# Second norm from ScalarE squares, gate batch by batch, batch 0 in the attention tail

## The chip, the core and the metric

The kernel runs on one core of a Trainium2 chip, in one launch. The metric is the device time of that core in microseconds (us). Of the kernel before, three runs gave 1397.35, 1399.73 and 1400.1 us, median 1399.73. The engines are named TensorE (PE), VectorE (DVE), ScalarE (ACT), GpSimd (POOL) and SyncE (SP, which only issues DMAs here).

## The reference, cut to what matters

Two blocks, each added to its input, over B = 4 batches of T = 1024 tokens of C = 128 features in float32.

```
x = x + attn(layernorm(x))            # 8 heads of differential attention, 16 score maps per batch
h = layernorm(x)                      # the second norm
logits = normalize(h) @ normalize(sim) - sigmoid(gates)        # 16 experts
gated  = relu(logits);  mask = gated > 0, or the top 2 where no expert is above 0
rw     = softmax(gated where mask, else -inf)                  # the routing weights
q, k, v = sum_e rw[e] * (h @ W[e])                             # 16 experts, 64 columns each
attn = causal softmax(q k^T / 8) v
x = x + sum_e rw[e] * (attn @ O[e])
```

The second norm needs the finished x of a token, and the gate needs the norm. The first expert product of a token needs its rw.

## The kernel before, in words

The program of each engine is written out by hand, in order, and semaphores join them. An engine whose next instruction waits does nothing behind it.

**Attention** (part one) runs over 256 units (batch, head, block of 128 queries), 32 slots in each of 8 iterations. Per unit TensorE makes two score maps of 128x1024, VectorE takes two negated row maxima (`row_max`, L1246), ScalarE two exponentials (L925), GpSimd scales and adds the two maps (`mix`, L488 and L490; of every eight units ScalarE scales two, L966), TensorE transposes the sum in eight blocks (L632), ScalarE and VectorE copy the two halves out (L854, L332), and TensorE multiplies by the values (L638). Per half of 512 tokens there is a chain: `rows` (transposes), copies and squares, `last`-stage sums, a root on three engines, `norm` on GpSimd (L510), `cols`, `project` (L692), and the addition to `resid` on VectorE (L1278). The slots run on for 21 more after the last unit, to empty this chain.

**Between the parts** the second norm is made for batches 0 to 2 together in those last slots (`ln2_early`): VectorE sums `resid` (L1201), makes the means (L1220), GpSimd and VectorE subtract them (L531, L1204), ScalarE squares 128x1024 at a time (L911), VectorE sums the squares (L1208), then the root and the scaling (L538, L1211). Batch 3 follows when its last half is added. The gate then runs once over all four batches: transposes (`t_ps`, `s_ps`, L721), their split into a float16 high and low part (L991, L1302), the logits (L712), and on VectorE the maxima of each of 32 tiles (L1349), their indices (L1352), the mask and the softmax, up to `rw_all` (L1375). The expert weights are loaded by SP after the last `resid` addition, scaled and split by ScalarE (L1003, L1006) and GpSimd (L548).

**Part two** runs over 32 tiles of 128 tokens. GpSimd multiplies a tile by its 16 weights (`scale_by_experts`, L557, two buffers `xs`: tile m waits for the low part of tile m - 2), ScalarE makes the high part (`x_high`, L1012), VectorE the low part (`x_low`, L1379), SP transposes both by DMA (L427), TensorE multiplies by the 16 experts in four groups (L761), then causal attention one tile behind and two behind, and the output product `y_ps` (L799) four tiles behind. On each engine the steps of several tiles stand in one fixed order per tile; ScalarE's begins with `x_high` of tile m + 2 and the copy of `qkT` (L1032), VectorE's with `x_low` of tile m + 2, and it ends with the low part of `qs` (L1437, L1439), for which TensorE waits at the start of tile m + 1.

Of the kernel before, what the change touches and what calls it, by code (L numbers as in the profile page):

```python
# [40 lines left out]
F16 = mybir.dt.float16  # L41
# [52 lines left out]
EARLY = 3  # L94
POOL_BATCHES = (0, 1)
LN2_SLOT = SLOTS + 1
BT = EARLY * NT
# [50 lines left out]
def block_kernel(nc, x, wq, wkv, wout, lq1, lk1, lq2, lk2, gamma, sim, gates, eq, ek, ev, eo, out):  # L148
    ctx = ExitStack()
    with ctx:  # L150
# [8 lines left out]
        def sem(name):  # L159
# [26 lines left out]
        x2c = prob2.rearrange("p b (t c) -> p (b t) c", c=C)  # L186
        x2sq = prob1[:, 0:4, :]
# [43 lines left out]
        gl = sb("gl", [P, 10, B * NT, E])  # L231
# [3 lines left out]
        rw_all = sb("rw_all", [P, B * NT, E])  # L235
        xs = sb("xs", [P, 2, E, C])
        ew_split = sb("ew_split", [P, 2, E, 3 * DE], F16)
        eow_split = sb("eow_split", [P, 2, E // 2, C], F16)
        xsT = sb("xsT", [P, X_BUFS, 2, E, P], F16)
        kv2 = sb("kv2", [P, NT, 2 * DE])  # L240
        kv_first = sb("kv_first", [P, 2 * DE])
        qs = sb("qs", [P, 2, 3, P], F16)
        qkT = sb("qkT", [P, 3, T], F16)
        p2 = prob2[:, 2:4, :]
        p2T = sb("p2T", [P, NT, P])
        nm2 = sb("nm2", [P, 2])
        sum2 = sb("sum2", [P, 2])
        rec2 = sb("rec2", [P, 2])
        mx = prob2[:, 0:2, :].rearrange("p r (e d) -> p r e d", d=DE)
# [34 lines left out]
        g_sum, g_mean, g_cP, g_cV, g_sq, g_ss, g_y, g_scale, g_nP, g_nV, g_T, g_A, g_V, g_lg, g_v, g_exp, rw_ok = (  # L284
            sem("g_" + n) for n in ("sum", "mean", "centred_P", "centred_V", "sq", "ss", "y", "scale", "normed_P",
                                    "normed_V", "T", "A", "V", "lg", "v", "exp", "rw"))
# [8 lines left out]
        GLATE, GNORM, GEXP = 6, 13, 22  # L295

        def gate_ps(n, half):

            return (t_ps[:, half, :], s2_ps[:, half * 512:(half + 1) * 512])[n % 2]

        def act_scaled(units):

            return sum(n % 8 in ACT_SCALES for n in range(units))
# [35 lines left out]
        def _(sp):  # L339
# [74 lines left out]
            sp.wait_ge(resid_ok, 2 * STEPS)  # L414
# [6 lines left out]
            def transpose_x(tile):  # L421
                r, buf = tile % 2, tile % X_BUFS
                if tile >= X_BUFS:
# [20 lines left out]
        def _(pool):  # L444
# [69 lines left out]
            def units(h, tail):  # L514

                for u in range(8):
                    mix(8 * h + u, (8 * h + u) % PROBS)
# [10 lines left out]
            pool.wait_ge(g_mean, 1)  # L528
            pool.wait_ge(mix_ok, STEPS * UNITS)
            for b in POOL_BATCHES:  # L530
                pool.tensor_tensor(x2c[:, b * NT:(b + 1) * NT, :], resid[:, b * NT:(b + 1) * NT, :],  # L531
                                   tokens(gs[:, 1, b * NT:(b + 1) * NT]), ALU.add).then_inc(g_cP, 1)
            root(2 * STEPS - 2)
            norm(2 * STEPS - 2)
            pool.wait_ge(g_cP, 2)
            pool.wait_ge(g_scale, 1)
            for b in POOL_BATCHES:
                pool.tensor_tensor(x2n[:, b * NT:(b + 1) * NT, :], x2c[:, b * NT:(b + 1) * NT, :],  # L538
                                   tokens(gs[:, 6, b * NT:(b + 1) * NT]), ALU.mult).then_inc(g_nP, 1)
            root(2 * STEPS - 1)  # L540
            norm(2 * STEPS - 1)


            pool.wait_ge(resid_ok, 2 * STEPS)

            for n, (w, split_w) in enumerate(((ew, ew_split), (eow, eow_split))):
                pool.wait_ge(w_hi, n + 1)
                pool.tensor_tensor(split_w[:, 1, :, :], w[:, :, :], split_w[:, 0, :, :], ALU.subtract).then_inc(w_lo, 1)  # L548
            pool.wait_ge(g_nP, 2)
            pool.wait_ge(g_nV, 2)  # L550
            pool.wait_ge(rw_ok, 1)

            def scale_by_experts(m, r, peeled):

                if m >= 2:
                    pool.wait_ge(xs_lo, m - 1)
                pool.tensor_tensor(xs[:, r, :, :], x2n[:, bass.ds(m, 1), :].to_broadcast([P, E, C]),  # L557
                                   rw_all[:, bass.ds(m, 1), :].rearrange("p a e -> p e a").to_broadcast([P, E, C]),
                                   ALU.mult).then_inc(xs_ok, 1)

            scale_by_experts(0, 0, True)
            scale_by_experts(1, 1, False)
            for pair in range(1, B * NT // 2):
                scale_by_experts(2 * pair, 0, False)
                scale_by_experts(2 * pair + 1, 1, False)
# [3 lines left out]
        def _(pe):  # L569
# [44 lines left out]
            def slots(it, first, last):  # L614
                end = SLOTS - 8 + TAIL_SLOTS if last else SLOTS
# [86 lines left out]
            pe.wait_ge(resid_ok, 2 * STEPS)  # L702
            pe.wait_ge(mask_ok, 6)

            def gate_logits(n):

                pe.wait_ge(g_V, 2 * (n + 1))
                if n == 0:
                    pe.wait_ge(c2_v, C2V)
                for t in range(NT):  # L710
                    for k, (x_part, w_part) in enumerate(SPLIT_PRODUCTS):
                        mm = pe.matmul(qkv_ps[:, (n * NT + t) * E:(n * NT + t + 1) * E], x2T[:, n % 2, x_part, t * P:(t + 1) * P],  # L712
# [3 lines left out]
            for n in range(B):  # L716
                pe.wait_ge(*((g_nP, n + 1) if n in POOL_BATCHES else (g_nV, n - 1)))
                if n >= 2:
                    pe.wait_ge(g_V, 2 * (n - 1))
                for t in range(NT):  # L720
                    mm = pe.transpose(gate_ps(n, t // 4)[:, t % 4 * P:(t % 4 + 1) * P], x2n[:, n * NT + t, :], ident[:, :])  # L721
                    if t % 4 == 3:
                        mm.then_inc(g_T, 1)
                if n:
                    gate_logits(n - 1)
            gate_logits(B - 1)
            pe.wait_ge(w_lo, 2)
            pe.wait_ge(rw_ok, 1)
            pe.wait_ge(g_V, 2 * B)

            def tiles2(it, first, last):
                for t in range(NT + PART2_LAG if last else NT):
# [16 lines left out]
                    def experts(group):  # L749
# [5 lines left out]
                        if group == 0 and not (first and t == 0):  # L755
                            pe.wait_ge(hi2, 2 * m)
                            pe.wait_ge(lo2, 2 * m)
                            pe.wait_ge(kv_read, m)
                        for e in range(4 * group, 4 * group + 4):
# [33 lines left out]
                    if live(4):  # L793
                        pe.wait_ge(mT_lo, 2 * (m - 3))
                        if not (first and t == 4):
                            pe.wait_ge(y_done, m - 4)
# [17 lines left out]
                    if live(1):  # L814
                        v = (t - 1) % NT
                        pe.wait_ge(qkt_ok, m)
                        if not (first and t == 1):
                            pe.wait_ge(exp2, m - 1)
# [9 lines left out]
                    experts(1)  # L828
                    if live(2):
# [13 lines left out]
                    experts(3)  # L843

# [7 lines left out]
        def _(act):  # L852
# [54 lines left out]
            def ln2_squares(b):  # L907
                act.wait_ge(*((g_cP, b + 1) if b in POOL_BATCHES else (g_cV, b - 1)))
                if b == 0:
                    act.wait_ge(trans_ok, 2 * STEPS * UNITS)  # L910
                act.activation(x2sq[:, b, :], x2c[:, b * NT:(b + 1) * NT, :].rearrange("p t c -> p (t c)"),  # L911
                               ACT.Square).then_inc(g_sq, 1)

            def slots(it, first, last):
                end = SLOTS - 8 + TAIL_SLOTS if last else SLOTS
# [554 lines left out]
```

## Time and profile before

| | |
|---|---|
| median of three runs | 1399.73 us |
| the profiled execution, whole | 1397.11 us |
| its span, first to last instruction | 1394.9 us |
| granted TensorE clock, mean | 0.973 |
| busy: PE, DVE, ACT, POOL | 87%, 85%, 79%, 74% |

The span in 40 equal slices, each digit the busy share in tenths (9 is 90% or more), PEclk the granted clock in tenths of full speed:

```profile
PE   2789999999999999999999999998862599999997
PEld 1344444444444444444444444444431498989897
DVE  5899999999999999999999999999858576767674
ACT  3899999999999999999999999999833455656553
POOL 3788898899989889998988999899942744434320
PEclk9899999999999999999999999999975799999999
```

Slices 1 and 2 are the start, up to slice 29 is attention, slices 30 to 32 are the passage between the parts, and from 33 on part two runs. Attention has all four engines busy at once; in the passage all four fall; part two has TensorE alone near its full share.

### The profile page before, as it was taken

What the parts mean: (1) busy time and instruction counts of PE and PEld (TensorE: products, weight loads), DVE (VectorE), ACT (ScalarE), POOL (GpSimd) and SP (SyncE); (2) the same over time, 40 slices, a digit from 0 to 9 for tenths busy, and PEclk for the clock granted to TensorE, in tenths of its full rate; (3) what the DMA queues carried; (4) which work ended last, traced back from release to release, by engine and by line L of the source; (5) the groups of instructions that cost most, each with busy time, mean ns of one, the idle gap of its engine ahead of it and who ended that gap; (6) DMA issues with size and microseconds to landing.
All of it is one profiled execution on the core that took longest, in us unless ns stands there. A gap on an engine that the chain in (4) does not pass through costs nothing. (4 is left out here: it accounts for less than half of the span.)

```text
span 1394.9 us, 24022 instructions
## 1 busy us (share of the span) xinstructions
PE 1219.2 (87%) x8370; PEld 748.1 (54%) x8370; DVE 1187.9 (85%) x1937; ACT 1101.6 (79%) x2031; POOL 1027.0 (74%) x714
## 2 busy tenths in 40 slices
PE   2789999999999999999999999998862599999997
PEld 1344444444444444444444444444431498989897
DVE  5899999999999999999999999999858576767674
ACT  3899999999999999999999999999833455656553
POOL 3788898899989889998988999899942744434320
PEclk9899999999999999999999999999975799999999
DMA  4232111121211112121111212110003876768570
GB/s 112 70 89 63 48 37 51 31 56 44 62 47 39 52 31 55 42 66 42 42 52 31 55 41 65 35 31 1 1 6 55 151 130 120 137 112 146 100 130 10
DMA packets 184598, 86.85 MB, mean 62 GB/s; under 512 B 150176, under 2 KB 166048, under 8 KB 184480
## 3 DMA queue, kind: packets, MB, share of 16 engines
q1 hardware_dynamic: 184480, 85.33, 28.8%
q8 instruction: 68, 1.11, 0.3%
q14 instruction: 50, 0.41, 0.1%
HBM read 7.68 MB, written 2.10 MB: 7 GB/s over the span
## 5 line engine op out<-in xcount | busy, mean ns | idle before, releaser
L1246 DVE TENSOR_REDUCE negmax<-score_ps 128x1 f32<-128x1024 f32 x512 | 617.8, 1217 | 47.8 <-PE score_ps L609 45.8
L490 POOL TENSOR_TENSOR prob<-prob 128x1024 f32<-128x1024 f32 x256 | 603.6, 2358 | 50.4 <-ACT prob L966 34.4
L925 ACT ACTIVATE prob<-score_ps,negmax 128x1024 f32<-128x1024 f32 x512 | 571.1, 1118 | 61.5 <-DVE negmax L1246 60.7
L609 PE MATMUL score_ps<-ka,qa 128*128 128x512 f16 x1024 | 307.9, 383 | 83.5 <-ACT prob L925 72.1
L638 PE MATMUL attn_ps<-probT,v_sb 128*64 128x512 f32 x1024 | 276.0, 619 | 0.8 <-ACT attn_nT L973 0.8
L632 PE MATMUL trans_ps<-ident,prob 128*128 128x128 f32 x2048 | 269.3, 274 | 0.8 <-POOL prob L490 0.3
L632 PEld LDWEIGHTS trans_ps<-ident,prob 128*128 128x128 f32 x2048 | 238.4, 141 | 56.2 <-issue 2.0
L557 POOL TENSOR_TENSOR xs<-xnT,rw_all 128x2048 f32<-128x2048 f32 x32 | 117.4, 3671 | 147.3 <-DVE prob L1379 140.5
L488 POOL TENSOR_SCALAR prob<-prob,ccol 128x1024 f32<-128x1024 f32 x192 | 215.2, 1121 | 3.3 <-DVE ccol L1259 3.3
L609 PEld LDWEIGHTS score_ps<-ka,qa 128*128 128x128 f16 x1024 | 80.5, 97 | 218.5 <-ACT prob L925 151.9
L332 DVE COPY probT<-trans_ps 128x512 f32<-128x512 f32 x256 | 174.1, 680 | 1.8 <-PE trans_ps L632 1.8
L761 PE MATMUL qkv_ps<-ew_split,xsT 128*128 128x192 f16 x1536 | 143.6, 248 | 32.9 <-DMA xsT<-prob 32.9
L854 ACT ACTIVATE probT<-trans_ps 128x512 f32<-128x512 f32 x256 | 154.1, 602 | 18.4 <-PE trans_ps L632 18.3
L761 PEld LDWEIGHTS qkv_ps<-ew_split,xsT 128*128 128x128 f16 x1536 | 127.8, 98 | 36.1 <-issue 33.0
L1379 DVE TENSOR_TENSOR prob<-xs,prob 128x2048 f16<-128x2048 f32 x32 | 78.4, 2451 | 49.0 <-ACT prob L1012 49.0
L638 PEld LDWEIGHTS attn_ps<-probT,v_sb 128*64 128x64 f32 x1024 | 51.1, 135 | 108.3 <-issue 108.3
L925 ACT ACTIVATION_READ_ACCUMULATOR prob<-score_ps,negmax 128x1 f32 x512 | 103.5, 202 | 0.0
L1049 ACT ACTIVATE prob<-s_ps,nm 128x128 f32<-128x128 f32 (+7 forms) x32 | 23.7, 741 | 69.2 <-DVE nm L1414 69.2
L1259 DVE TENSOR_SCALAR ccol<-recip,sums,lam 128x1 f32<-128x1 f32 x256 | 69.9, 273 | 9.4
L1012 ACT ACTIVATE prob<-xs 128x2048 f16<-128x2048 f32 x32 | 61.5, 1921 | 16.8 <-POOL xs L557 16.8
L966 ACT ACTIVATE prob<-prob,ccol 128x1024 f32<-128x1024 f32 x64 | 72.8, 1137 | 0.0
L587 PE MATMUL misc_ps<-xg,wg 128*128 128x512 f32 x120 | 67.5, 645 | 2.4 <-DVE split L1165 2.4
(195 smaller groups left out, 1321.5 us busy)
## 6 DMA issues: line engine op xcount, KB each, us to landing
qa<-split SPq DMA_DIRECT2D x256, 64.0 KB, 2.0
ka<-split SPq DMA_DIRECT2D x256, 64.0 KB, 2.0
xg<-xnT SPq DMA_DIRECT2D x16, 512.0 KB, 3.0
resid<-in_L_attn_x SPq DMA_DIRECT2D x4, 512.0 KB, 6.3
wg<-in_L_attn_Wkv SPq DMA_DIRECT2D x32, 64.0 KB, 2.0
out<-prob SPq DMA_DIRECT2D x32, 64.0 KB, 2.6
wg<-in_L_attn_Wq SPq DMA_DIRECT2D x16, 64.0 KB, 1.9
xsT<-prob SPq DMA_TRANSPOSE x64, 4.5
```

What stands on the lines that cost most here:

```text
L332: copy(probT[:, half % 2, 4 * bank:4 * bank + 4, u // 4, (u % 4) * P:(u % 4 + 1) * P], trans_ps[:, bank, :].rearrange("p (k q) -> p k q", ...
L488: pool.tensor_scalar(prob2[:, n % 4, :], prob2[:, n % 4, :], ccol[:, u:u + 1], 1.0, ALU.mult, ALU.mult).then_inc(scaled_P, 1)
L490: pool.tensor_tensor(prob1[:, n % PROBS, :], prob1[:, n % PROBS, :], prob2[:, n % 4, :], ALU.add).then_inc(mix_ok, 1)
L557: pool.tensor_tensor(xs[:, r, :, :], x2n[:, bass.ds(m, 1), :].to_broadcast([P, E, C]), rw_all[:, bass.ds(m, 1), :].rearrange("p a e -> p e ...
L609: mm = pe.matmul(score_ps[:, sub, kh * HALF:(kh + 1) * HALF], qa[:, par, head * 2 + sub, q0:q0 + P], ka[:, par, head * 2 + sub, kh * HALF: ...
L632: mm = pe.transpose(trans_ps[:, kb, t * P:(t + 1) * P], prob1[:, (n - TRANS_LAG) % PROBS, k0:k0 + P], ident[:, :])
L638: return pe.matmul(attn_ps[head * DV:(head + 1) * DV, :], v_sb[:, (half // 2) % 2, kt, head * DV:(head + 1) * DV], probT[:, half % 2, kt, ...
L761: mm = pe.matmul(qkv_ps[:, 0:3 * DE], xsT[:, t % X_BUFS, x_part, e, :], ew_split[:, w_part, e, :], start=e == 0 and n == 0, stop=e == E - ...
L854: return act.activation(dst, src, ACT.Copy)
L925: act.activation(prob2[:, n % 4, :] if sub else prob1[:, n % PROBS, :], score_ps[:, sub, :], ACT.Exp, bias=negmax[:, s % 2, sub:sub + 1], ...
L1246: dve.tensor_reduce(negmax[:, s % 2, sub:sub + 1], score_ps[:, sub, :], AX.X, ALU.max, negate=True).then_inc(max_ok, 1)
L1379: dve.tensor_tensor(xs_split[:, r, 1, :, :], xs[:, r, :, :], xs_split[:, r, 0, :, :], ALU.subtract).then_inc(xs_lo, 1)
```

## The change

Squares and sums of batches 0 to 2 move into the last two iterations of attention. VectorE makes sum and mean of a batch in each of three slots (`SUM_SLOTS`, all at a multiple of eight); ScalarE squares one tile of 128x128 at a time with the mean as its bias and the sum as its accumulator (24 tiles in ten slots, `SQUARE_SLOTS`; seven of them take three tiles, at slot 4 of eight, and three take one). The centred copy and its sums fall away, and the scaling becomes one VectorE `tensor_scalar` per tile with two pointer scalars (`ln2_normed`). The expert weights are loaded as soon as the buffers under them are free, inside attention. The slots after the last unit end after four; the rest of the emptying is written out by hand, interleaved with the gate of batch 0. The last unit's sum moves from GpSimd to ScalarE (scale) and VectorE (add). Batches 1 to 3 have their gate in part two, with the steps after the indices on GpSimd; batch 3 has its norm there too.

```
-EARLY = 3
-POOL_BATCHES = (0, 1)
+SUM_SLOTS = {(ITERS - 2, 8): 0, (ITERS - 2, 16): 1, (ITERS - 2, 24): 2}
+SQUARE_SLOTS = {(ITERS - 2, 12): (0, 3), (ITERS - 2, 20): (3, 6), (ITERS - 2, 24): (6, 7), (ITERS - 2, 28): (7, 10),
+                (ITERS - 1, 4): (10, 13), (ITERS - 1, 12): (13, 16), (ITERS - 1, 16): (16, 17), (ITERS - 1, 20): (17, 20),
+                (ITERS - 1, 24): (20, 21), (ITERS - 1, 28): (21, 24)}
+LAST_SLOTS = SLOTS + TRANS_LAG
...
SyncE
-            sp.wait_ge(resid_ok, 2 * STEPS)
+            sp.wait_ge(filled["v1"], STEPS)
+            for kind in "qk":
+                sp.wait_ge(stacked[kind], 256 * (STEPS - 1) + 128)
...
GpSimd, after attention
+            pool.wait_ge(g_scale, 1)
+            weights_low(0)
+            pool.wait_ge(g_sub, 1)
+            weights_low(1)
+            root(HALVES - 2)
+            norm(HALVES - 2)
+            scale_by_experts(0)
+            weights_low(2)
+            scale_by_experts(1)
+            gate_logit(1)
+            gate_logit(2)
+            root(HALVES - 1)
+            scale_by_experts(2)
+            pool.wait_ge(cols_ok, HALVES - 1)
+            norm(HALVES - 1)
+            gate_chosen(1)
+            scale_by_experts(3)
+            pool.wait_ge(w_hi, 4)
+            pool.tensor_tensor(eow_split[:, 1, :, :], eow[:, :, :], eow_split[:, 0, :, :], ALU.subtract).then_inc(w_lo, 1)
+            gate_kept(1)
+            scale_by_experts(4)
+            ln2_mean()
+            scale_by_experts(5)
+            ln2_variance()
+            ln2_root()
+            gate_weights(1)
+            scale_by_experts(6)
+            norm_root()
+            gate_chosen(2)
+            scale_by_experts(7)
+            gate_kept(2)
...
TensorE, after attention
+            last_values(0)
+            pe.wait_ge(exp_ok, 2 * STEPS * UNITS)
+            gate_transposes(0)
+            pe.wait_ge(resid_ok, HALVES - 2)
+            transposed_rows(attnT, misc_ps)
+            last_values(1)
+            last_values(2)
+            gate_logits(0)
+            for kt in range(3, 6):
+                last_values(kt)
+            pe.wait_ge(attn_copied, 2 * (HALVES - 1))
+            columns(HALVES - 2)
+            last_values(6)
+            last_values(7)
+            project(HALVES - 2)
+            pe.wait_ge(attnT_ok, HALVES)
+            transposed_rows(attnT_last, trans_ps[:, 1, :])
+            gate_transposes(1)
+            gate_transposes(2)
+            gate_logits(1)
+            gate_logits(2)
...
+                if m == 0 and group == 1:
+                    pe.wait_ge(resid_ok, HALVES - 1)
+                    columns(HALVES - 1)
+                elif m == 0 and group == 3:
+                    project(HALVES - 1)
+                elif m == 2 and group == 3:
+                    pe.wait_ge(resid_ok, HALVES)
+                    gate_transposes(3)
+                elif m == 3 and group == 3:
+                    gate_logits(3)
...
ScalarE
-            def ln2_squares(b):
-                act.wait_ge(*((g_cP, b + 1) if b in POOL_BATCHES else (g_cV, b - 1)))
-                act.activation(x2sq[:, b, :], x2c[:, b * NT:(b + 1) * NT, :].rearrange("p t c -> p (t c)"),
-                               ACT.Square).then_inc(g_sq, 1)
+            def ln2_squares(m0, m1):
+                act.wait_ge(g_mean, (m1 - 1) // NT + 1)
+                for m in range(m0, m1):
+                    act.activation(x2n[:, m, :], resid[:, m, :], ACT.Square, bias=gs[:, 1, m:m + 1],
+                                   accum_out=gs[:, 7, m:m + 1]).then_inc(g_sq, 1)
...
+            weights_scaled(1)
+            gate_high(0)
+            seed(0, g_nrm, 2)
+            weights_high(1)
+            rows_copies(HALVES - 2, misc_ps[:, :])
+            root_seed(HALVES - 2)
+            weights_high(2)
+            columns_copy(HALVES - 2)
+            gate_exp(0)
+            act.activation(eow[:, :, :], eow[:, :, :], ACT.Copy, scale=WSCALE).then_inc(w_scaled, 1)
+            act.wait_ge(pv_ok, 8 * HALVES)
+            act.wait_ge(mix_ok, STEPS * UNITS)
+            act.activation(attnT_last, attn_ps[:, :], ACT.Copy).then_inc(attnT_ok, 1)
+            gate_high(1)
+            rows_copies(HALVES - 1, trans_ps[:, 1, :])
+            x_high(0, 0)
+            gate_high(2)
+            root_seed(HALVES - 1)
+            act.wait_ge(w_scaled, 3)
+            act.activation(eow_split[:, 0, :, :], eow[:, :, :], ACT.Copy).then_inc(w_hi, 1)
+            x_high(1, 1)
+            columns_copy(HALVES - 1)
...
+            def extra(m):
+                if m == 0:
+                    gate_exp(1)
+                elif m == 1:
+                    ln2_squares(3 * NT, 4 * NT)
+                    seed(1, g_var, 0)
+                elif m == 2:
+                    seed(1, g_nrm, 2)
+                    gate_high(3)
...
VectorE
+            def ln2_mean(b):
+                ln2_sum(b)
+                dve.wait_ge(g_sum, b + 1)
+                dve.tensor_scalar(per_tile(1, b), per_tile(0, b), -1.0 / C, None, ALU.mult).then_inc(g_mean, 1)
+            def ln2_normed(b):
+                for m in range(b * NT, (b + 1) * NT):
+                    dve.tensor_scalar(x2n[:, m, :], resid[:, m, :], gs[:, 1, m:m + 1], gs[:, 0, m:m + 1],
+                                      ALU.add, ALU.mult).then_inc(g_n, 1)
...
+            dve.wait_ge(g_scale, 1)
+            ln2_normed(0)
+            norm_squares()
+            gate_low(0)
+            norm_root()
+            gate_read(0)
+            last_stat(HALVES - 2)
+            gate_top(0)
+            last_root(HALVES - 2)
+            gate_chosen(0)
+            gate_weights(0)
+            last_add(HALVES - 2)
+            ln2_normed(1)
+            ln2_normed(2)
+            gate_low(1)
+            gate_read(1)
+            last_stat(HALVES - 1)
+            x_low(0, 0)
+            gate_low(2)
+            gate_read(2)
+            last_root(HALVES - 1)
+            gate_top(1)
+            x_low(1, 1)
+            gate_top(2)
...
+            def extra(m):
+                if m == 0:
+                    last_add(HALVES - 1)
+                    ln2_sum(3)
+                elif m == 2:
+                    gate_sums(1)
+                    ln2_normed(3)
+                elif m == 3:
+                    gate_low(3)
+                elif m == 4:
+                    gate_read(3)
+                elif m == 6:
+                    gate_sums(2)
+                elif m == 8:
+                    gate_top(3)
+                elif m == 12:
+                    gate_sums(3)
```

ScalarE calls its `extra(m)` at the end of tile m, VectorE its own behind `x_low` of tile m + 2. `gate_chosen(b)` on GpSimd is a chain of 13 instructions: four over 8 or 16 elements, nine over 128.

## Rows read from the trace of the kernel before

**Rows 1.** Busy time by stretch (us): engine busy (instructions), granted clock, DMA share, GB/s.

```profile
885.80:1007.90 122.10, 111.05 (x621) 57.08 (x620) 113.47 (x178) 113.18 (x208) 112.02 (x82) 1.00 0.08 18
1007.90:1044.10 36.20, 24.46 (x120) 12.42 (x117) 18.38 (x29) 12.75 (x26) 20.11 (x21) 0.83 0.00 1
1044.10:1093.20 49.10, 9.76 (x128) 8.57 (x129) 36.27 (x139) 18.01 (x20) 19.85 (x5) 0.53 0.38 69
1093.20:1120.90 27.70, 22.20 (x228) 20.21 (x229) 18.98 (x19) 13.70 (x29) 18.51 (x6) 0.94 1.00 178
1120.90:1394.90 274.00, 257.68 (x2989) 242.29 (x2989) 184.11 (x283) 147.41 (x295) 87.11 (x25) 1.00 0.63 109
```

**Rows 2.** Timeline of the passage: start, duration (us), engine, line, instruction, count, idle before.

```profile
1007.71 0.19 ACT L925 ACTIVATION_READ_ACCUMULATOR prob<-score_ps,negmax 128x1 f32 x1
...
1013.16 2.36 POOL L490 TENSOR_TENSOR prob<-prob 128x1024 f32<-128x1024 f32 x1
...
1078.34 0.69 DVE L1375 TENSOR_TENSOR rw_all<-gl,gs 128x512 f32<-128x512 f32 x1
...
1079.20 7.17 POOL L557 TENSOR_TENSOR xs<-xnT,rw_all 128x2048 f32<-128x2048 f32 x2 [6.77 <-DVE rw_all L1375]
...
1082.84 1.91 ACT L1012 ACTIVATE prob<-xs 128x2048 f16<-128x2048 f32 x1 [9.20 <-POOL xs L557]
...
1084.85 5.87 DVE L1379 TENSOR_TENSOR prob<-xs,prob 128x2048 f16<-128x2048 f32 x2 [5.82 <-ACT prob L1012]
...
1093.20 5.84 PE L761 MATMUL qkv_ps<-ew_split,xsT 128*128 128x192 f16 x48 [32.91 <-DMA xsT<-prob]
1100.38 0.33 PE L809 MATMUL qk_ps<-identh,qs 128*128 128x128 f16 x3 [1.33 <-DVE qs L1439]
...
1120.88 1.51 PE L799 MATMUL y_ps<-eow_split,mxT 128*128 128x128 f16 x24 [0.20 <-DVE mxT L1430]
```

**Rows 3.** Timeline of attention, around the end of a slot 4 of eight.

```profile
785.40 0.23 ACT L925 ACTIVATION_READ_ACCUMULATOR prob<-score_ps,negmax 128x1 f32 x1
785.60 1.12 ACT L925 ACTIVATE prob<-score_ps,negmax 128x1024 f32<-128x1024 f32 x1
...
786.16 1.04 PE L632 MATMUL trans_ps<-ident,prob 128*128 128x128 f32 x8
787.04 0.59 PE L609 MATMUL score_ps<-ka,qa 128*128 128x512 f16 x2
```

**Rows 4.** Timeline of ScalarE in part two: a 128x128 exponential with an accumulator.

```profile
1105.97 0.37 ACT L1049 ACTIVATE prob<-s_ps,nm 128x128 f32<-128x128 f32 x1 [4.15 <-DVE nm L1414]
1106.23 0.19 ACT L1049 ACTIVATION_READ_ACCUMULATOR prob<-s_ps,nm 128x1 f32 x1
1106.33 0.30 ACT L1064 ACTIVATE kv<-kv_first 128x128 f32<-128x128 f32 x1
```

**Rows 5.** Timeline of sums and means of the second norm, and of GpSimd's mix.

```profile
771.75 2.37 POOL L490 TENSOR_TENSOR prob<-prob 128x1024 f32<-128x1024 f32 x1
...
1011.28 3.46 DVE L1201 TENSOR_REDUCE gs<-resid 128x8 f32<-128x1024 f32 x3
1014.78 0.77 DVE L1220 TENSOR_SCALAR gs<-gs 128x24 f32<-128x24 f32 x1
...
1045.38 0.17 DVE L1310 TENSOR_SCALAR gs<-gs 128x8 f32<-128x8 f32 x1
```

**Rows 6.** Timeline of GpSimd and VectorE in the gate.

```profile
1070.31 2.12 POOL L548 TENSOR_TENSOR eow_split<-eow,eow_split 128x1024 f16<-128x1024 f32 x1
...
1070.43 2.55 DVE L1356 SCALAR_TENSOR_TENSOR gl<-gl,gs 128x512 f32<-128x512 f32 x1
```

**Rows 7.** Timeline of short instructions and of a weight split.

```profile
1022.98 0.20 POOL L496 TENSOR_TENSOR tl<-tl 128x8 f32<-128x8 f32 x1 [2.52 <-ACT tl L960]
1023.26 0.20 POOL L498 TENSOR_TENSOR tl<-tl 128x8 f32<-128x8 f32 x1
...
1061.78 2.54 DVE L1349 MAX8 top<-gl 128x8 f32<-128x16 f32 x32
...
1064.36 5.99 POOL L548 TENSOR_TENSOR ew_split<-ew,ew_split 128x3072 f16<-128x3072 f32 x1 [25.05 <-ACT ew_split L1006]
```

More of the change, by code:

```diff
@@ L540, in _, with weights_low @@
[L540 to L546, printed above, removed]
-                pool.wait_ge(w_hi, n + 1)
[L548 to L553, printed above, removed]
+            def weights_low(n):
+                e0, e1 = W_PARTS[n]
+                pool.wait_ge(w_hi, n + 1)
+                pool.tensor_tensor(ew_split[:, 1, e0:e1, :], ew[:, e0:e1, :], ew_split[:, 0, e0:e1, :], ALU.subtract).then_inc(w_lo, 1)
@@ new lines, in _ @@
+            gate_kept(1)
[10 more added lines that the diff above has]
+            gate_kept(2)
+            for m in range(8, B * NT):
+                scale_by_experts(m)
+                if m == 8:
+                    gate_weights(2)
+                elif m == 9:
+                    gate_logit(3)
+                elif m == 11:
+                    gate_chosen(3)
+                elif m == 13:
+                    gate_kept(3)
+                elif m == 15:
+                    gate_weights(3)
@@ L614, in slots @@
             def slots(it, first, last):
-                end = SLOTS - 8 + TAIL_SLOTS if last else SLOTS
+                end = LAST_SLOTS if last else SLOTS
                 if first:
@@ L699, in _, with last_values @@
             slots(ITERS - 1, False, True)
[L702 to L708, printed above, removed]
+            def last_values(kt):
+                for head in range(2):
+                    mm = pe.matmul(attn_ps[head * DV:(head + 1) * DV, :], v_sb[:, 1, kt, head * DV:(head + 1) * DV],
+                                   probT[:, 1, kt, head, :], start=kt == 0, stop=kt == 7)
+                mm.then_inc(pv_ok, 1)
@@ new lines, in project, with gate_transposes @@
+            def project(h):
+                pe.wait_ge(attn_nT_ok, h + 1)
+                for t in range(4):
+                    mm = pe.matmul(misc_ps[:, t * P:(t + 1) * P], attn_nT[:, t, :], wo_sb[:, G - 1, :], start=True, stop=True)
+                mm.then_inc(out_ok, 1)
+            def gate_transposes(b):
+                pe.wait_ge(g_n, NT * (b + 1))
+                if b == 2:
+                    pe.wait_ge(g_V, 2)
+                elif b == 3:
+                    pe.wait_ge(g_V, 6)
+                for t in range(NT):
+                    mm = pe.transpose(gate_ps(b, t // 4)[:, t % 4 * P:(t % 4 + 1) * P], x2n[:, b * NT + t, :], ident[:, :])
+                    if t % 4 == 3:
+                        mm.then_inc(g_T, 1)
@@ L794, in tiles2 @@
                         pe.wait_ge(mT_lo, 2 * (m - 3))
-                        if not (first and t == 4):
+                        if m == 4:
+                            pe.wait_ge(w_lo, 4)
+                        else:
                             pe.wait_ge(y_done, m - 4)
@@ L1281, in slots @@
                         row_max(n + 1, s + 1, 0)
+                    if last and s == SLOTS + 2:
+                        last_mix()
                     copy_probT(dve, dve.tensor_copy, s, n, it, 1, first, last)
@@ new lines, in gate_top @@
+            def gate_top(b):
+                if b == 0:
+                    dve.tensor_tensor(rows(gl[:, 0, :, :], b), rows(gl[:, 1, :, :], b), per_expert(sgate[:, :]),
+                                      ALU.subtract).then_inc(g_sub, 1)
+                dve.wait_ge(g_sub, b + 1)
+                for t in range(b * NT, (b + 1) * NT):
+                    dve.max(out=top8[:, t, :], in_=gl[:, 0, t, :]).then_inc(g_top, 1)
+                dve.wait_ge(g_top, tops(b) + NT)
+                for t in range(b * NT, (b + 1) * NT):
+                    dve.max_index(out=top8i[:, t, :], in_max=top8[:, t, :], in_values=gl[:, 0, t, :]).then_inc(g_top, 1)
```

462 lines of the change are left out of this document (277 added, 185 removed).

## The prediction

> **What bounds the kernel now.** I read the busy time by stretch first, then the timelines of all engines through the passage between the parts. The reader sees three regimes in [rows 1]. In attention all four engines are over 90% busy: in the last 122.1 us PE 111.0, DVE 113.5, ACT 113.2, POOL 112.0. So nothing added there is free by itself. In the passage, 1007.9 to 1093.2, PE works 34.2 of 85.3 us, at a granted clock of 0.83 and then 0.53. From 1120.9 on PE is busy 257.7 of 274.0 us and the other engines far less. Part two, once filled, is bound by TensorE, and what is saved before it moves the end one for one. The passage is a chain [rows 2]: last exponential done at 1007.90, last mixed unit at 1015.52, routing weights at 1079.03, first scaled tile, its high and low part, its DMA, first expert matmul at 1093.20. The first four tiles then take until 1120.88, where the first output product starts: 27.7 us. Below, E is the end of the last exponential; before, the first expert matmul stands at E + 85.3 and the first output product at E + 113.0.
>
> **Squares in attention: +4.4 us.** 24 squares of 128x128 with an accumulator. The nearest instruction is a 128x128 exponential with an accumulator: start to start of the next 1106.33 - 1105.97 = 0.36 us [rows 4]. Seven slots take three, 1.08 us each. Behind a slot 4, ScalarE's next exponential starts 0.1 us after ScalarE could take it, and the score matmul that it releases is held 0.24 us longer by the transposes in front of it [rows 3]: slack 0.34, so 0.74 us pass on. I count six such groups (4.4) and nothing for the seventh, near the end, nor for the three single squares, which I place in slots with more idle. Bounds 0 (they fit into ScalarE's 8.9 us of idle in the last 122.1, [rows 1]) and 24 x 0.36 = 8.6.
>
> **Sums and means in attention: +6.7 us.** Three sums, 3.46/3 = 1.15 each, up to 1.22 by itself, and three means of 0.17 [rows 5]. They stand on VectorE ahead of a row maximum that ScalarE waits for, so I pass on all of the 1.39. The mean is a small SBUF-to-SBUF instruction, and the rows show such a one waiting: 1014.78 took 0.77 us and ended at 1015.55, just when the mix of 1013.16 ended [rows 2, 5]; with GpSimd idle it took 0.17. In the gate a VectorE instruction of 1070.43 ended 0.55 after GpSimd's of 1070.31 did [rows 6]. GpSimd is 92% busy in attention, with instructions of 1.1 to 2.4 us, so a mean falls into one and waits 0.85 us on average: 3 x (1.39 + 0.85) = 6.7. Bounds 3 x 1.39 = 4.2 without a wait, 3 x (1.39 + 1.75) = 9.4 if each mean comes 0.6 us into a mix of 2.37, as the place of [rows 5] suggests.
>
> **The passage to the routing weights of batch 0: at E + 25.5, before E + 71.1.** Durations are those of the same instructions before.
> - The last unit is added on VectorE (1.2) right after unit 254, at E + 5.4 for E + 7.6. Its transposes stand behind a projection on TensorE (7.3 to 8.3), its copies end at 9.0.
> - GpSimd splits the first half of the weights, 5.99/2 = 3.0 [rows 7], from 7.5 to 10.5. `ln2_normed(0)`, eight pointer instructions at 0.175 each (from the 0.17 of rows 5), waits for that: 11.9.
> - Transposes 1.0, two high copies, two low parts: 14.5. The root's five steps 1.1, the logits behind two value products at 16.4, read and sums to 17.6, then 8 maxima at 0.08 [rows 7] and 8 indices: 19.7. GpSimd splits again from 17.9 (1.5), then its root of five at 0.28 [rows 7], to 20.9.
> - The mask chain 2.4 plus about 1.1 behind the `norm` on GpSimd, then 1.1: 25.5.
>
> The loads of the weights move into attention, past no other DMA that is still to be waited for; I cost them at nothing. Before, they and the scaling were hidden under the gate too.
>
> **To the first expert matmul: E + 44.0, 41.3 us earlier.** GpSimd's first tile takes 3.6 [rows 2], to 29.1. VectorE then runs 16 pointer instructions (2.8) to 32.0; I take it that this string, which has no wait in it, keeps GpSimd out. GpSimd follows with 1.5 + 3.6, to 37.1. ScalarE's high part of tile 0 is done at 35.4 behind two copies of batch 1 and the rows of the last half; VectorE's low part waits for GpSimd's 37.1 and takes 2.2 (the 5.87 of [rows 2] is a wait until 1086.37 and two of 2.18): 39.3. The DMA takes as before 1093.20 - 1088.55 = 4.65: 44.0.
>
> **The first four tiles: 50.0 us for 27.7, 22.3 us given back.** GpSimd's queue sets the pace.
> - Logits 42.5, root 43.9, tile 2 to 47.5, wait for the low part of tile 1 (2.2), `norm` of the last half: 50.8. TensorE stands inside tile 0 for it; the projection ends near 57; VectorE adds it and sums batch 3 (1.9) before the low part of `qs`: tile 1 starts at about 59, 15 us after tile 0, before 7.2 [rows 2].
> - `gate_chosen(1)`: 13 steps at 0.28 plus nine times 128 elements at 5.99/3072 = 0.25 [rows 7]: 5.9, and 2.2 behind a low part: 58.9. Tile 3's scaling 62.5, its high part 64.4, then ScalarE copies `qkT`: TensorE ends tile 1 at 68.2.
> - ScalarE's squares of batch 3 wait for GpSimd's mean (behind 2.1 + 2.2 + 0.5 + 3.6: 71.2), its seed for the variance behind another tile (75.1). High part and `qkT` come at 78.0, tile 2 ends at 81.8.
> - `ln2_normed(3)` 81.7, transposes 82.9; low part of `qs` 84.0; tile 3 needs `gate_high(3)`, a high part and `qkT` (87.1): its logits end at 93.0, and the first output product starts at E + 94.0.
>
> **Later: +1.0 us.** The remaining gate steps (maxima of batch 3, 1.9, sums, a read) are VectorE's, which has 90 us of idle in the 274 [rows 1]; if that cover were gone they cost about 4.
>
> **Sum.** 1397.1 - 41.3 + 22.3 + 4.4 + 6.7 + 1.0 = 1390.2 against the profiled execution. The median of the runs lies 2.6 above that execution, so 1392.8, say 1393 us.
>
> **Rivals.**
> 1. *The port, taken in turns* (slower). Place: VectorE's strings against GpSimd's long instructions. If after each pointer instruction GpSimd gets the next turn, batch 1 is normed at 35.8 for 30.6, which makes the first matmul 3.3 later; `ln2_normed(3)` straddles a tile's scaling (+4.0); each mean waits the full 1.75 (+2.7); later low parts wait for gate steps (+2): +12, so 1405 us, and with all squares passing on (+4.2) 1409. It is slower than before once these waits pass 7. For it: both waits named above ended with GpSimd's instruction. Against: no row shows a VectorE string without waits against two GpSimd instructions. The Trainium skill, page "SBUF — State Buffer", section "Who interferes with whom", says that a VectorE instruction with two SBUF inputs, or in a two-port mode such as `tensor_scalar` can have, and a GpSimd one exclude each other for a whole instruction, and whoever issues first has the port. The two rows agree with it; by it, every change of hands costs a full instruction, which is this rival.
> 2. *The start keeps its gain.* If the first tiles take no more than before, plus TensorE's added 3.5 (transposes, logits and projection), the sum is 1393 - 22.3 + 3.5 = 1374. For it: no engine is full in that stretch before. Against: the order of GpSimd's queue.
> 3. *Half clock.* The clock is 0.53 in the passage and rises once TensorE works densely [rows 1]. If the stalls of tiles 0 to 3 keep it at the lower level (1.2 for 2.4 GHz), about 10 us of their 22 lie on the path twice: 1403.
> 4. *VectorE does not wait for GpSimd at all* in these instructions: 2.5 less in attention and 8.5 less up to the first output product: 1382. The waits in rows 5 and 6 speak against it.
>
> **How the numbers follow.** The forecast has 0.38, rival 1 0.25, rival 2 0.12, rival 3 0.08, rival 4 0.07; 0.10 stays for the changes eating up each other, at about no difference. About 0.2% (2.8 us) is what a measurement can tell from none. Faster: 0.32 of the forecast, 0.12 + 0.07, and 0.02 of the unnamed tenth: 0.53. Same: 0.04 of the forecast, 0.04 of rival 1, 0.02 and 0.05: 0.15. Slower: 0.21 of rival 1, 0.06 of rival 3, 0.02 of the forecast and 0.03: 0.32. The range reaches from 1376, nearly rival 2, to 1409, rival 1 with its bound; the forecast's own is 1386 to 1399, its square and sum terms at their ends and 4 us of play in the queue of the first tiles.
>
> **What would show it.** In the changed profile: the last exponential 11 us later than 1007.9; a mean of 128x8 in attention that lasts longer than 0.17; the first expert matmul 44 us after the last exponential and the first output product 50 us after that; GpSimd without gaps between. It is wrong if attention ends within 3 us of 1007.9, or if the first four tiles take under 35 us.

## The result, and the profile after

| | before | after |
|---|---|---|
| median of four runs each | 1399.84 us | 1427.38 us |
| profiled execution: span | 1394.9 us | 1422.6 us |
| mean granted clock | 0.973 | 0.972 |

The ratio is 1.0201, 95% interval 1.0189 to 1.0213: 28 us slower, where 7 us faster was forecast, and outside the range (1376 to 1409).

The same slices of the page as before the change:

```profile
PE   2789999999999999999999888988954788899997
DVE  5899999999999999999999989899874767667675
ACT  2899999999999999999999888999943454455553
POOL 3788988998988898898899888888848543534320
PEclk9899999999999999999999999999987899899999
```

The hole of the passage is narrower, but the start of part two is thinner: in slices 33 to 35 PE shows 8 where it had 9, while attention, with 8s from slice 23 on, runs longer. By stretch (the last 122.1 us of attention, the passage to the first expert matmul, the first four tiles, the next 113.5 us, the rest), to be laid beside [rows 1]:

```profile
901.69:1023.79 122.10, 108.52 (x609) 55.77 (x608) 110.43 (x173) 115.02 (x231) 109.13 (x80) 1.00 0.18 35
1023.79:1072.70 48.91, 27.33 (x204) 15.58 (x202) 36.30 (x107) 24.64 (x40) 22.44 (x22) 0.83 0.14 27
1072.70:1124.48 51.78, 30.92 (x272) 27.57 (x272) 31.27 (x78) 19.83 (x55) 44.55 (x48) 0.80 0.58 98
1124.48:1238.00 113.52, 95.02 (x1016) 88.40 (x1017) 73.60 (x125) 51.97 (x104) 47.70 (x31) 0.91 0.59 100
1238.00:1422.60 184.60, 171.02 (x1977) 160.53 (x1974) 120.94 (x188) 95.44 (x191) 50.54 (x14) 1.00 0.57 100
```

E, the end of the last exponential, is 1023.79. The terms of the sum, each from the starts of the same instructions in both traces:

| term | forecast | measured | from |
|---|---|---|---|
| start, before the first moved instruction | 0 | +1.2 | unit 186: 744.56 for 743.34 |
| squares, sums and means in attention | +11.1 | +14.7 | E later by 15.9, less 1.2 |
| first expert matmul after E | -41.3 | -36.4 | E + 48.9 for E + 85.3 |
| first four tiles | +22.3 | +24.1 | 51.8 for 27.7 |
| later | +1.0 | +24.1 | first output product to the end |
| sum | -6.9 | +27.7 | the spans differ by 27.7 |

The forecast missed by 34.6 us in all, and the last term holds 23.1 of them. Output product y n belongs to tile n and comes in TensorE's tile n + 4. The time from one to the next (differences of their starts in the timelines), in us, with the kernels of the experiments beside it:

| to y | before | after | e1 | e5 | e6 | e7 | e8 |
|---|---|---|---|---|---|---|---|
| 1 | 8.01 | 12.02 | 12.03 | 12.04 | 8.39 | 8.39 | 8.39 |
| 2 | 8.44 | 8.60 | 8.60 | 8.60 | 9.77 | 9.79 | 8.30 |
| 3 | 9.29 | 14.42 | 9.63 | 9.64 | 10.91 | 10.91 | 9.63 |
| 4 | 9.78 | 10.29 | 10.57 | 10.57 | 10.52 | 10.51 | 10.79 |
| 5 | 10.14 | 12.04 | 12.03 | 13.69 | 17.76 | 10.48 | 10.48 |
| 6 | 10.49 | 14.27 | 14.57 | 11.31 | 17.92 | 10.93 | 10.93 |
| 7 | 8.12 | 8.12 | 8.32 | 8.32 | 8.81 | 8.81 | 8.82 |
| 8 | 7.50 | 7.50 | 7.50 | 7.50 | 8.05 | 8.04 | 8.04 |
| 9 | 8.30 | 16.74 | 8.85 | 8.86 | 8.23 | 8.23 | 8.23 |

From y 10 on before and after agree within 0.3 us each. The loss to y 3 and y 9 is one event that comes twice. The timeline after, at tile 6 (start, duration, engine, line, instruction, idle before it and its releaser):

```profile
1145.55 0.32 ACT L1227 ACTIVATE gl<-gl 128x128 f32<-128x128 f32 x1
1145.94 0.46 POOL L654 TENSOR_TENSOR gl<-gl 128x128 f32<-128x128 f32 x1 [17.21 <-ACT gl L1227]
1146.36 3.61 POOL L564 TENSOR_TENSOR xs<-xnT,rw_all 128x2048 f32<-128x2048 f32 x1
1150.06 1.91 ACT L1254 ACTIVATE prob<-xs 128x2048 f16<-128x2048 f32 x1 [4.19 <-POOL xs L564]
1151.88 0.47 ACT L1309 ACTIVATE qkT<-qk_ps 128x384 f16<-128x384 f16 x1
1152.40 0.61 PE L1030 MATMUL s_ps<-qkT 128*128 128x512 f16 x1 [4.09 <-ACT qkT L1309]
```

Read it upwards. TensorE's scores wait for `qkT`, which stands on ScalarE behind the high part of tile 8, which waits for GpSimd's `scale_by_experts(8)`. That tile's inputs were long there; it stands in GpSimd's queue behind `gate_kept(2)`, and this waited 17.2 us for an exponential of 0.32 us, which ScalarE has at the end of its tile 5. A wait of 17 us on an engine with time to spare would cost nothing; the instruction queued behind it is the next tile. At 1212.70 the same happens with batch 3 (19.9 us).

The losses to y 1 and y 6 (4.0 and 3.8 us) have another place. To y 1, the 13 gate steps of `gate_chosen(2)` on GpSimd push a tile's scaling back until it meets VectorE's low part:

```profile
1125.12 3.61 POOL L564 TENSOR_TENSOR xs<-xnT,rw_all 128x2048 f32<-128x2048 f32 x1
1125.71 5.17 DVE L1672 TENSOR_TENSOR prob<-xs,prob 128x2048 f16<-128x2048 f32 x1 [0.96 <-ACT prob L1254]
...
1131.25 1.45 PE L1046 MATMUL o_ps<-kv,p2T 128*128 128x128 f32 x6 [2.30 <-issue]
```

The low part starts 0.6 us behind the scaling and takes 5.17 us instead of 2.29: it ends 2.15 us after the scaling does, about its own length. TensorE's next step stands behind VectorE's, and TensorE idles 2.3 us. To y 6 it is the same behind the gate steps of batch 3 (1.0 us behind, 4.73 us, TensorE idle 3.4 us). To y 5 (1.9 us) the search of batch 3, 2 us of VectorE, stands ahead of a copy for which TensorE idles 2.1 us.

### The profile page after: what moved, and what is told of

Its sections match the earlier page's. It is cut to its first block and busy times, and to the rows that moved or that the text cites. A ratio compares the mean times of both kernels' runs of the same rounds, so it can differ in the third digit from the quotient of the medians.

```text
span 1422.6 us, 24199 instructions
## 1 busy us (share of the span) xinstructions
PE 1232.9 (87%) x8370; PEld 757.0 (53%) x8370; DVE 1201.0 (84%) x1966; ACT 1109.8 (78%) x2100; POOL 1046.8 (74%) x772
## 3 DMA queue, kind: packets, MB, share of 16 engines
q8 instruction: 68, 1.11, 0.3%
## 5 line engine op out<-in xcount | busy, mean ns | idle before, releaser
L776 PE MATMUL attn_ps<-probT,v_sb 128*64 128x512 f32 x992 | 267.5, 618 | 0.0
L964 PE MATMUL qkv_ps<-ew_split,xsT 128*128 128x192 f16 x1536 | 151.2, 255 | 3.1 <-DMA xsT<-prob 3.1
L964 PEld LDWEIGHTS qkv_ps<-ew_split,xsT 128*128 128x128 f16 x1536 | 134.3, 102 | 7.6 <-issue 3.4
L1672 DVE TENSOR_TENSOR prob<-xs,prob 128x2048 f16<-128x2048 f32 x32 | 82.4, 2574 | 59.0 <-ACT prob L1254 59.0
```

Source lines behind the costliest of these rows:

```text
L776: return pe.matmul(attn_ps[head * DV:(head + 1) * DV, :], v_sb[:, (half // 2) % 2, kt, head * DV:(head + 1) * DV], probT[:, half % 2, kt, ...
L964: mm = pe.matmul(qkv_ps[:, 0:3 * DE], xsT[:, t % X_BUFS, x_part, e, :], ew_split[:, w_part, e, :], start=e == 0 and n == 0, stop=e == E - ...
L1672: dve.tensor_tensor(xs_split[:, r, 1, :, :], xs[:, r, :, :], xs_split[:, r, 0, :, :], ALU.subtract).then_inc(xs_lo, 1)
```

## The experiments

e1 to e4, e5 and e6, and e7 and e8 ran on one chip each; each ratio is to the kernel before on the same chip. The changed kernel's four runs lie between 1424.1 and 1430.6 us and its traced one at 1424.6, so a gain read in the traces can be up to 3 us smaller than that of the medians.

**e1: the exponentials of gates 2 and 3 two tiles earlier.**

```
 def extra(m):                     # ScalarE
-    elif m == 5:  gate_exp(2)
+    elif m == 3:  gate_exp(2)
-    elif m == 11: gate_exp(3)
+    elif m == 9:  gate_exp(3)
```

> ScalarE issues gate_exp(2) at the end of its tile 3 instead of tile 5 and gate_exp(3) at the end of tile 9 instead of tile 11; nothing else moves. Theory (the tiles lose where GpSimd stands in gate_kept and waits for an exponential that is queued late on ScalarE: 17.2 us at tile 6 and 19.9 us at tile 12, so that scale_by_experts of tiles 8 and 14 come late): GpSimd waits under 2 us in both, the interval before first y 3 loses about 5.1 us less and the one before y 9 about 8.4 us less, together -9 to -13 us against the changed kernel (1427.4 to about 1415). Rival (the loss comes from GpSimd holding the shared read path against VectorE's x_low, or from the low granted clock of these tiles, and would only move to another tile): within 3 us of the changed kernel.

1413.41 us, ratio 1.0107 (1.0080 to 1.0133). The intervals to y 3 and y 9 lose 4.8 and 7.9 less; 0.8 of that is lost again in others. The same place in this kernel, GpSimd's wait gone and the tile 14.7 us earlier:

```profile
1124.29 0.35 ACT L1227 ACTIVATE gl<-gl 128x128 f32<-128x128 f32 x1
...
1129.25 2.50 POOL L654 TENSOR_TENSOR gl<-gl 128x128 f32<-128x128 f32 x1
1131.71 3.60 POOL L564 TENSOR_TENSOR xs<-xnT,rw_all 128x2048 f32<-128x2048 f32 x1
```

One `gate_kept` still waited 4.6 us (under 2 expected), at little cost: 8.85 to y 9 for 8.30 before. Two lines moved in one queue are half of the late loss.

**e2: the three means on ScalarE.**

```
-                dve.wait_ge(g_sum, b + 1)
-                dve.tensor_scalar(per_tile(1, b), per_tile(0, b), -1.0 / C, None, ALU.mult).then_inc(g_mean, 1)
+                        act.wait_ge(g_sum, b + 1)
+                        act.activation(gs[:, 1, b * NT:(b + 1) * NT], gs[:, 0, b * NT:(b + 1) * NT], ACT.Copy, scale=-1.0 / C).then_inc(g_mean, 1)
```

> The means of batches 0 to 2 are computed by ScalarE from VectorE's sums (a copy with scale -1/C at the end of the slot after) instead of by VectorE's tensor_scalar right behind the sum. Theory (the mean is a pointer-free tensor_scalar that waits until GpSimd's mix lets go of the shared path, so that each of slots 8, 16 and 24 is held up by 2.9 us): each of the three places loses about 1.4 us instead of 2.9 us, -4 to -5 us at the last exponential and at the end. Rival (the sum alone already pays for the wait, or the next VectorE instruction, a row maximum, pays in its place): the three places keep their 2.9 us, within 1 us.

1417.56 us, ratio 1.0134 (1.0118 to 1.0151). In the changed kernel, the sum and the mean beside GpSimd's mix:

```profile
802.89 1.21 DVE L1480 TENSOR_REDUCE gs<-resid 128x8 f32<-128x1024 f32 x1
803.52 2.35 POOL L512 TENSOR_TENSOR prob<-prob 128x1024 f32<-128x1024 f32 x1
804.13 1.77 DVE L1485 TENSOR_SCALAR gs<-gs 128x8 f32<-128x8 f32 x1
807.44 1.11 ACT L1150 ACTIVATE prob<-score_ps,negmax 128x1024 f32<-128x1024 f32 x1 [3.33 <-DVE negmax L1551]
```

and in e2, where ScalarE then waits 1.54 instead of 3.33:

```profile
802.25 1.21 DVE L1485 TENSOR_REDUCE gs<-resid 128x8 f32<-128x1024 f32 x1
802.87 2.35 POOL L513 TENSOR_TENSOR prob<-prob 128x1024 f32<-128x1024 f32 x1
...
805.00 1.11 ACT L1151 ACTIVATE prob<-score_ps,negmax 128x1024 f32<-128x1024 f32 x1 [1.54 <-DVE negmax L1554]
```

The mean of eight numbers ends with the mix (804.13 + 1.77 = 805.90; 803.52 + 2.35 = 805.87). Each place costs 1.13 us for 2.92: the sum passes on nearly its whole length, the mean a further 1.8. Counted from unit 186, as in the table above, the last exponential comes 5.4 earlier, a little over what was expected; the interval to y 1 gave 1.7 more, and why is open.

**e3: the squares one by one.** Ends of slots 0 and 6 and the place ahead of the second exponential take one square each; the groups of three go.

```
-SQUARE_SLOTS = {(ITERS - 2, 12): (0, 3), (ITERS - 2, 20): (3, 6), (ITERS - 2, 24): (6, 7), (ITERS - 2, 28): (7, 10),
...
+SQUARE_ENDS = [(ITERS - 2, 14, 1), (ITERS - 2, 16, 3), (ITERS - 2, 22, 6), (ITERS - 2, 24, 8), (ITERS - 2, 30, 11), (ITERS - 1, 0, 13),
...
+SQUARE_MIDS = [(ITERS - 2, 11, 0), (ITERS - 2, 15, 2), (ITERS - 2, 17, 4), (ITERS - 2, 19, 5), (ITERS - 2, 23, 7), (ITERS - 2, 25, 9),
...
```

> The 24 squares run one by one, at ends of slots and ahead of the second exponential where ScalarE was seen waiting, instead of in groups of up to three. Theory (a group of three outlasts the slack of its slot by about 1 us, a single one does not): the last exponential comes 4 to 6 us earlier than in the changed kernel and the end with it. Rival (ScalarE's work is on the path of every slot, so that 24 squares cost 24 times a quarter of a microsecond wherever they stand): within 1.5 us.

1422.73 us, ratio 1.0174 (1.0157 to 1.0191). Counted from unit 186, the last exponential is 4.1 earlier, as the theory has it. The end is not clear of the changed kernel's, whose interval (1.0189 to 1.0213) this one touches. In the changed kernel two squares take 889.67 - 888.90 = 0.77 us from start to start, so a group of three takes about 1.16:

```profile
888.90 0.43 ACT L1120 ACTIVATE xnT<-resid,gs 128x128 f32<-128x128 f32 x1
...
889.67 0.41 ACT L1120 ACTIVATE xnT<-resid,gs 128x128 f32<-128x128 f32 x1
```

and passed on 1.04 to 1.06 per group (the last one 0.58), of which about 0.13 came back each time. In e3 single squares cost nothing in most places, but unit 211 loses 1.33 and unit 239 0.35. In e5, where the means are on ScalarE too, unit 211 loses nothing and unit 239 still does; why is open.

**e4: GpSimd's `weights_low(2)` behind VectorE's 24 normalized tiles.**

```
             scale_by_experts(0)
+            pool.wait_ge(g_n, 3 * NT)
             weights_low(2)
```

> GpSimd's weights_low(2) waits until VectorE has issued all 24 normalized tiles of batches 0 to 2. Theory (in the passage behind attention VectorE's 16 pointer instructions take 9.7 us instead of about 3.8 because they take turns with three GpSimd instructions): the 16 take 6 to 7.5 us, the first expert matmul stands 2 to 4 us earlier against the last exponential (46 instead of 48.9), and the end moves by -3 to +2 us, since GpSimd's own string is pushed back. Rival (VectorE's pace there does not depend on GpSimd): the 16 still take over 9 us and the first expert matmul is not earlier.

1423.68 us, ratio 1.0185 (1.0168 to 1.0202). In the changed kernel the 16 pointer instructions of batches 1 and 2 stand among three of GpSimd:

```profile
1049.70 3.61 POOL L564 TENSOR_TENSOR xs<-xnT,rw_all 128x2048 f32<-128x2048 f32 x1 [3.49 <-DVE rw_all L1668]
1052.16 9.72 DVE L1502 TENSOR_SCALAR xnT<-resid,gs 128x128 f32<-128x128 f32 x16
1053.27 1.64 POOL L555 TENSOR_TENSOR ew_split<-ew,ew_split 128x768 f16<-128x768 f32 x1
1054.86 3.61 POOL L564 TENSOR_TENSOR xs<-xnT,rw_all 128x2048 f32<-128x2048 f32 x1
```

With GpSimd held back:

```profile
1051.19 5.10 DVE L1503 TENSOR_SCALAR xnT<-resid,gs 128x128 f32<-128x128 f32 x16
1056.37 1.64 POOL L555 TENSOR_TENSOR ew_split<-ew,ew_split 128x768 f16<-128x768 f32 x1 [4.00 <-DVE xnT L1503]
```

5.10 us is less than the 6 to 7.5 expected. The first expert matmul stands 3.4 nearer to the last exponential. The median is 3.7 us under the changed kernel's, but its interval and this one overlap, so a gain at the end of the run is not shown.

**e5: the four together.**

> The four edits of the first experiments together (exponentials of gates 2 and 3 two tiles earlier on ScalarE, means on ScalarE, single squares, weights_low(2) behind the normalized tiles). Theory (four separate losses that add up): 14.0 + 9.8 + 4.7 + 3.7 less than the changed kernel, minus the 1.7 that the second and the fourth both won in the interval before y 1, so 1427.4 - 30.5 = 1397, about the kernel before. Rival (they won the same time, or the attention pieces win only once): 1403 or more.

1399.63 us, ratio 1.0003 (0.9993 to 1.0013): 2.6 above the 1397 expected and under the rival's 1403. The losses nearly add up, and four small moves take the whole slowdown back. The first four tiles still take 52.8 us.

**e6: the gates spread out.** On top of e5, batch 3's squares, roots, transposes and logits run in tiles 4 to 12 and its top-8 search and remaining gate steps up to tile 18; GpSimd's list of gate steps is cut in two; half 31's (the last half's) norm, columns and projection stand later. The exponentials of gates 2 and 3 go along, to the ends of tiles 5 and 14. The core of GpSimd's queue:

```
+            scale_by_experts(4)
+            gate_chosen_a(1)
...
+            scale_by_experts(5)
+            gate_chosen_b(1)
+            scale_by_experts(6)
+            gate_kept(1)
...
```

> As the four together, and no gate's work in one piece any more: batch 3's squares, roots, transposes and logits run in expert tiles 4 to 12 instead of 0 to 4, each list of gate steps on GpSimd is cut in two with a scale_by_experts between, the top-8 search of batches 1 and 2 stands behind x_low, and half 31's norm, columns and projection run one tile later. Theory (what is left of the loss behind the first y, about 9 us, and the long first four tiles, 51.8 us against 27.7 before, come from GpSimd's gate pieces standing ahead of scale_by_experts): first four tiles 36 to 42 us, the intervals before y 1 to y 9 within 3 us of the kernel before in sum, time about 1375. Rival (the first tiles are long because TensorE runs at the low granted clock there and the intervals because VectorE and GpSimd share a path, wherever the pieces stand): first four tiles 47 us or more, time 1388 or more.

1401.27 us, ratio 1.0014 (1.0004 to 1.0023). The kernel that ran lacks the wait of e4, so its 16 pointer instructions took 8.8 again (4.2 in e5). The first four tiles took 38.7, as expected, and the first output product came 10.3 earlier than in e5. But the intervals to y 1 to y 9 lose 20.3 to the kernel before, not 3, and 15.1 of it is in y 5 and y 6. The timeline there:

```profile
1145.10 2.29 DVE L1702 TENSOR_TENSOR prob<-xs,prob 128x2048 f16<-128x2048 f32 x1 [1.64 <-ACT prob L1280]
...
1147.31 4.50 DVE L1530 TENSOR_SCALAR xnT<-resid,gs 128x128 f32<-128x128 f32 x4
1147.48 3.64 POOL L569 TENSOR_TENSOR xs<-xnT,rw_all 128x2048 f32<-128x2048 f32 x1 [4.98 <-DVE prob L1702]
...
1151.94 0.54 DVE L1783 COPY p2T<-t_ps 128x384 f32<-128x384 f32 x1
...
1152.58 3.33 PE L1066 MATMUL o_ps<-kv,p2T 128*128 128x128 f32 x14 [4.96 <-issue]
```

The end of the low part releases GpSimd's next tile and VectorE's four pointer instructions in the same moment. The first gets in ahead of GpSimd, the second takes 3.63 us (in both groups; the median of the eight is 0.34), and the copy that TensorE needs stands behind them. TensorE idles 5 us, and its granted clock over tiles 8 and 9 (1147.31 to 1182.00) is 0.80, between the levels of 1.2 and 2.4 GHz, where it was 1.00 in the 25 us before. So the theory held for the first four tiles and failed for the intervals, whose loss had moved to a new place.

**e7: those four ahead of the low part instead of behind it.**

```
+                    if m in (8, 9):
+                        ln2_normed(3, 4 * (m - 8), 4 * (m - 7))
                     if not (last and t + X_AHEAD >= NT):
                         x_low(m + X_AHEAD, t % 2)
```

> As the spread gates, with one thing moved: the two groups of four pointer instructions of ln2_normed(3) stand ahead of VectorE's x_low in tiles 8 and 9 instead of right behind it. Theory (behind x_low they meet the scale_by_experts that x_low has just released: the second of the four waited 3.6 us for it, VectorE's row maximum and copy stand behind, TensorE waited 5 us for the copy and then ran at the low clock): the four take under 1.5 us, the intervals before y 5 and y 6 fall from 35.7 us together to 20.6 to 22, the time from 1401.3 to about 1387. Rival (these tiles are long from the transposes and copies of batch 3 or from the low clock that is there anyway): 30 us or more, time 1397 or more.

1385.16 us, ratio 0.9897 (0.9880 to 0.9913), 16 us less than e6, with eight instructions moved by one place. They fill the time in which VectorE waits for ScalarE's high part anyway:

```profile
1142.67 1.11 DVE L1530 TENSOR_SCALAR xnT<-resid,gs 128x128 f32<-128x128 f32 x4
...
1144.39 2.29 DVE L1702 TENSOR_TENSOR prob<-xs,prob 128x2048 f16<-128x2048 f32 x1 [0.62 <-ACT prob L1280]
...
1146.77 3.61 POOL L569 TENSOR_TENSOR xs<-xnT,rw_all 128x2048 f32<-128x2048 f32 x1 [4.99 <-DVE prob L1702]
...
1147.45 1.80 PE L1066 MATMUL o_ps<-kv,p2T 128*128 128x128 f32 x14 [0.54 <-issue]
```

The two intervals fell from 35.7 to 21.4, which is 14.3 us. The rest is not shown to be the edit's: the passage, which it leaves alone, took 2.3 us less in this trace than in e6's, with a granted clock of 1.00 for 0.90 in its first 16 to 17 us.

**e8: the rest out of the way.**

```
+            pool.wait_ge(g_n, 3 * NT)
             weights_low(2)
             scale_by_experts(1)
-            gate_logit(1)
             scale_by_experts(2)
-            gate_logit(2)
             root(HALVES - 1)
             scale_by_experts(3)
+            gate_logit(1)
+            gate_logit(2)
...
+                        if m in (4, 5, 6):        # ScalarE, ahead of the score exponential
+                            ln2_squares(3 * NT + 3 * (m - 4), min(3 * NT + 3 * (m - 3), 4 * NT))
```

> As the one before, and: weights_low(2) waits again behind the normalized tiles; root, logits and the reciprocal of half 31 stand behind x_low and scale_by_experts of the first tiles; batch 3's squares stand ahead of the score exponential (where ScalarE waited 2.0 to 2.8 us for VectorE's maximum) instead of ahead of x_high; the top-8 search of batch 3 stands ahead of x_low. Theory (each of these held the next scale_by_experts, x_high or x_low): first y 3 us earlier, the intervals before y 1 to y 14 about 4 us less in sum, time about 1380. Rival (they were hidden): within 2 us of the one before.

1380.02 us, ratio 0.9866 (0.9849 to 0.9882): 19 us faster than the kernel before and 47 than the changed one. The first output product stands 86.0 us after the start of the last exponential (88.8 in e7), the intervals to y 1 to y 14 lose 3.6 less. Its four parts were not run apart. Its first four tiles and the rest:

```profile
1056.89:1096.61 39.72, 28.79 (x239) 26.02 (x240) 27.80 (x73) 14.14 (x29) 38.20 (x30) 0.80 0.70 128
1096.61:1375.20 278.59, 259.56 (x3023) 243.85 (x3021) 190.40 (x322) 152.79 (x319) 106.69 (x69) 1.00 0.63 107
```

From the first output product on it takes 278.6 us against 274.0 in [rows 1], with the late gates inside.

## Why the prediction was wrong

1. **"Later: +1.0 us" is the step that failed: +24.1.** It counted the busy time of what was left for VectorE against VectorE's idle, and of GpSimd's and ScalarE's leftover steps not even that. The cost was not work but place. GpSimd's queue holds the next tile behind gate steps, and these wait for ScalarE's exponentials, which stand at the end of a tile (11.9 net, shown by e1). Most of the other half is read in the trace: gate steps make a tile's scaling late, so that it meets VectorE's low part on the port (to y 1 and y 6), and the search stands ahead of a copy (to y 5). e6 to e8 take out all but 3.5 of the loss up to y 9, but not each of these causes by itself. The order of all three queues was in the change, so this could have been followed as the first tiles were.
2. **Sums and means, +6.7: measured +8.8.** The average wait of 0.85 for the mean was the wrong choice; the place is fixed by the slot, and each falls into a mix at the same point. The upper bound, from the place in [rows 5], was near (2.92 for 3.14 each). e2 shows the cause.
3. **Squares, +4.4: measured about 5.9.** Right in kind (groups pass on, single squares don't, e3). A square takes 0.385, not 0.36 [rows 4], and the slack behind slot 4 was 0.1 (1.16 less 1.05), not 0.34, which is less than the 0.24 read off the transposes [rows 3] alone. The seventh group, put at nothing, passed on 0.58.
4. **Routing weights at E + 25.5: measured E + 25.8.** Right, by the steps of the list.
5. **First expert matmul at E + 44.0: measured E + 48.9.** The step that failed is that VectorE's string "keeps GpSimd out". It doesn't: the 16 took 9.72 us, the two engines in turn, and with GpSimd held back 3.4 of the 4.9 come back (e4). With no GpSimd instruction among them they take 4.2 (e5), 0.26 each from start to start, where 0.175 each and 2.8 in all was forecast. Taking turns is the mechanism of rival 1, which had it at 3.3. The Trainium skill, page "SBUF — State Buffer", section "Who interferes with whom", has the exclusive lock; the traces agree (in e6 4.50 us for four that take 1.11 in e7, with a 3.6 us instruction of GpSimd between the first and the second), and add that having issued first does not keep the port for the next instruction.
6. **First four tiles 50.0: measured 51.8.** Right, and for the reason given: GpSimd is busy 44.6 of 51.8 us. e6 shows it from the other side, with 38.7.
7. **The rivals.** Rival 1 named the right mechanism for point 5 and for the low parts behind y 0, but had only 2 us for the latter; the wait for the late exponentials was in none. Rival 3: the clock was 0.80 in the first four tiles and 0.91 in the next 113.5 us, where it had been 0.94 and 1.00 [rows 1]. With the stalls behind y 0 gone (e8) it is 1.00 there, so in that stretch it went with the stalls. In the first four tiles it is 0.80 in e8 too, and no run shows what that costs. Rival 2 fell with the 51.8 us of the first four tiles, rival 4 with the mean's 1.77 us beside the mix and with e4.

## What to carry to other kernels

When small steps are put into the queue of an engine with much idle, ask for each wait they bring which instruction stands behind it, and follow that one to the engine that sets the pace: two steps of 0.45 us cost 12 us here. Steps that share a resource with another engine belong where that engine is known to wait (ahead of the instruction that releases it), not right behind the release. Count a stage with all of its queues, also where its busy shares are low.

## What the runs showed of the hardware that was not expected

- The wait on the port goes both ways, and a tiny instruction can wait as long as a large one: in e4 a GpSimd instruction on 128x8 elements took 2.40 us beside VectorE's low part, which started 0.01 us earlier, where the four before it took 0.20 us each:

```profile
1101.14 2.29 DVE L1673 TENSOR_TENSOR prob<-xs,prob 128x2048 f16<-128x2048 f32 x1 [5.76 <-ACT prob L1255]
1101.15 2.40 POOL L610 TENSOR_SCALAR gs<-gs 128x8 f32<-128x8 f32 x1
```

- In the gate steps on GpSimd, on 128x128 elements, a compare with a constant (and a multiplication by 1 in the same instruction) takes longer than an operation on two tensors: 0.65 us for 0.41 to 0.46 (lines 646 and 648 against 644 and 649 after). In attention it is the other way: on 128x1024 elements a multiplication by scalars takes 1.12 us, an addition of two tensors 2.36.
